# A loop over three batches in all five engines, written out as straight-line code

## What is computed

```python
# layer 0, per batch
x = x + gate_s * (window_attention(modulate(ln(x))) @ w_so + b_so)        # 16 heads of 16, windows of 128, shifted by 64
x = x + gate_c * (topk_cross_attention(modulate(ln(x)), ctx) @ w_co + b_co)  # top 16 of 77 context tokens
x = x + gate_m * (swiglu(modulate(ln(x))) @ w_m2 + b_m2)                  # hidden width 1024
# layer 1, per batch
nx = layer_norm(x); ev = softmax(nx @ keys.T / 16) @ values               # keys, values from the context
h  = concat(nx, ev, cond)
y  = sum_e route[e] * (silu(h @ e_w1[e] + e_b1[e]) @ e_w2[e] + e_b2[e])   # 3 experts, softmax router
y  = y * sigmoid(silu(h @ gate_w1 + gate_b1) @ gate_w2 + gate_b2)
out = x + y @ out_w + out_b
```

## Time and profile before

| what | value |
|---|---|
| median of 3 runs | 1470.52 us (1466.71 to 1470.59) |
| the profiled execution, own time | 1472.61 us |
| its span, first to last instruction | 1470.8 us |
| PE busy | 1419.6 us (97%) |
| DVE, ACT, POOL busy | 69%, 57%, 29% |

### The profile page before, as it was taken

How to read it: one execution, slowest core, us unless ns; L and a number is a source line. 1 busy time by engine, 2 the same in 40 slices (tenths; PEclk the granted TensorE clock), 3 DMA queues, 4 the chain that set the end, 5 groups by cost and what they waited for, 6 DMA issues and landing times.

```text
span 1470.8 us, 33203 instructions
## 1 busy us (share of the span) xinstructions
PE 1419.6 (97%) x9701; PEld 1196.6 (81%) x9701; DVE 1019.0 (69%) x4629; ACT 840.8 (57%) x2554; POOL 427.6 (29%) x613
## 2 busy tenths in 40 slices
PE   6978999999999999999999999999999999999987
PEld 5856888888888788888888788888888888887876
DVE  3384858678695867869596686959587685958532
ACT  3364375756657475665747466574757547574423
POOL 2213232323225232322334232233234313232302
PEclk9878999999999999999999999999999999999989
DMA  7600000010000000010010000000010000000000
GB/s 240 234 30 1 1 1 25 1 34 9 19 30 7 12 2 25 2 33 2 12 45 2 17 2 16 11 14 21 9 47 2 15 2 8 2 2 8 1 8 8
DMA packets 27368, 35.26 MB, mean 24 GB/s; under 512 B 3324, under 2 KB 22448, under 8 KB 26929
## 3 DMA queue, kind: packets, MB, share of 16 engines
q1 hardware_dynamic: 27185, 33.07, 7.2%
HBM read 28.83 MB, written 4.22 MB: 22 GB/s over the span
## 4 chain that ended last, share of the span: by engine, by line
PE 81%; DVE 12%; issue 4%; ACT 2%; DVEq 0%; SPq 0%; DMA 0%; POOL 0%; ACTq 0%; POOLq 0%
PE bank L932 14%; PE bank L956 12%; PE bank L887 11%; PE bank L939 7%; PE bank L760 6%; PE bank L819 5%; PE bank L896 4%; PE bank L807 4%; PE bank L871 3%; DVE knocked L2125 3%; PE bank L746 3%; PE bank L799 2%; PE bank L717 2%; DVE M L2113 2%; PE bank L731 1%
## 5 line engine op out<-in xcount | busy, mean ns | idle before, releaser
L887 PE MATMUL bank<-hB,Wm 128*128 128x256 f32 x1024 | 243.8, 384 | 4.4 <-issue 3.1
L887 PEld LDWEIGHTS bank<-hB,Wm 128*128 128x128 f32 x1024 | 191.2, 191 | 36.5 <-issue 12.4
L932 PE MATMUL bank<-nxT,W1nx 128*128 128x256 f32 x896 | 214.7, 386 | 0.0
L1341 ACT ACTIVATE prob<-bank,rmax 128x128 f32<-128x128 f32 x512 | 180.4, 434 | 30.6 <-DVE rmax L2073 30.6
L1348 ACT ACTIVATE probT<-bank 128x512 f32<-128x512 f32 (+1 forms) x256 | 140.2, 616 | 91.1 <-PE bank L871 77.9
L1684 POOL TENSOR_TENSOR scores<-scores,M 128x308 f32<-128x308 f32 x128 | 94.4, 737 | 331.0 <-DVE knocked L2125 331.0
L932 PEld LDWEIGHTS bank<-nxT,W1nx 128*128 128x128 f32 x896 | 168.2, 193 | 24.0 <-issue 2.8
L956 PE MATMUL bank<-W2p,gT 128*128 128x256 f32 x768 | 184.6, 384 | 2.9 <-DVE acc L2204 1.9
L956 PEld LDWEIGHTS bank<-W2p,gT 128*128 128x128 f32 x768 | 141.9, 191 | 24.1 <-issue 2.8
L1377 ACT ACTIVATE tbs<-bank,b1half 128x256 f32<-128x256 f32 x128 | 60.7, 474 | 148.1 <-PE bank L887 99.3
L1389 ACT ACTIVATE tbs<-bank,betaH 128x256 f32<-128x256 f32 x224 | 95.6, 489 | 82.4 <-PE bank L939 82.4
(11 more groups left out here) (223 smaller groups left out, 2715.7 us busy)
## 6 DMA issues: line engine op xcount, KB each, us to landing
Wm_g<-in_L_xcond_w_m_dram SPq DMA_DIRECT2D x4, 1024.0 KB, 6.0
W1ev<-in_L_xcond_e_w_dram SPq DMA_DIRECT2D x6, 512.0 KB, 7.6
x<-in_x_dram SPq DMA_DIRECT2D x16, 128.0 KB, 2.2
x<-in_x_dram SPq DMA_DIRECT2D x32, 64.0 KB, 2.7
Wm<-in_L_xcond_w_m_dram SPq DMA_DIRECT2D x1, 2048.0 KB, 9.3
out_dram<-acc SPq DMA_DIRECT2D x16, 128.0 KB, 1.7
out_dram<-acc SPq DMA_DIRECT2D x32, 64.0 KB, 2.0
batch_rows<-row_store SPq DMA_DIRECT2D x4, 384.0 KB, 4.1
```

Of the source, the lines that this page charges most:

```text
L887: m = pe.matmul(bank_of(name)[:, half * UT:(half + 1) * UT], Wm1[:, k, c:c + P], hB[:, k, :], start=(k == 0), stop=(k == CB - 1))
L932: pe.matmul(bank_of(name)[:, n * UT:(n + 1) * UT], W1nx[:, k, c0 + n * P:c0 + (n + 1) * P], nxT[:, k, :], start=(n == 0 and k == 0), stop= ...
L1341: m = act.activation(prob[:, s, i, :], psum[s][:, i * P:(i + 1) * P], ACT.Exp, bias=rmax[:, t, s * HPS + i:s * HPS + i + 1], accum_out=rsu ...
```

## The change

The hardware loop becomes a Python loop in all five engines. The body is then emitted three times, q (or b) is 0, 1 and 2, and every wait value, DMA offset and batch index in it is a constant. Nothing else differs: the order of the work, the tiles, the semaphores, the prologue and the passes behind the loop are the same.

```diff
@@ SyncE
-            with sp.Fori(0, NB - 1) as b:
+            for b in range(NB - 1):
                 for r in range(1, UNITS + 1):
                     both(b * UNITS + r, r % UNITS, b)
                     load_x(b * UNITS + r + UNITS - 1, r - 1)
@@ TensorE
-            with pe.Fori(0, NB - 1) as q:
+            for q in range(NB - 1):
                 for r in range(1, UNITS + 1):
                     both(q * UNITS + r, r % UNITS, q + r // 3)
@@ ScalarE
-            with act.Fori(0, NB - 1) as q:
+            for q in range(NB - 1):
@@ GpSimd
-            with pool.Fori(0, NB - 1) as q:
+            for q in range(NB - 1):
@@ VectorE
-            with dve.Fori(0, NB - 1) as q:
+            for q in range(NB - 1):
```

## The result

The changed kernel takes 1466.32 us in the median of 20 runs (1460.61 to 1469.31), the kernel before 1471.07 us in 20 runs (1466.71 to 1475.45). The ratio is 0.9965, 95% interval 0.9955 to 0.9975: faster by 5.1 us, 3.7 to 6.6 us (the two medians are 4.75 us apart). I had forecast 1462.6 us, 7.9 us less. The direction was right and the time lies in the range, but about a third of the gain is missing.

The account below looks back on a forecast made before the run. PE, busy 97% of the span, was taken to bound the kernel. Returns of 3.46 us plus constants of 4.4 us gave 7.9 us off the 1470.52 us median: 1462.6 us, range 1458.0 to 1467.5 us.

Parts of the forecast that it names:

- What bounds it: Whole span: PE is busy 97% of it and carries 81% of the chain, so only waits of PE count.
- Part 1: PE before L887, at the loop's two returns: 1.71 and 1.75 us of issue wait go away, 3.46 us.
- Part 2: All loop passes: constant wait values end small delays, chiefly on DVE before its pick L2132; 4.4 us over three iterations.
- 0.15 us of r = 1: Loop passes with r = 1: what constants gain per pass beyond the return, 0.15 us in each of 3 passes.
- r = 2: Loop passes with r = 2, no return among them: constants gain 0.38 us each, 82.10 to 81.72 us.
- r = 3: Loop passes with r = 3, no twin behind the loop: gain bounded by nothing and 0.93 us, taken as 0.5 us.
- r = 0: Loop passes with r = 0, no twin behind the loop: gain bounded by nothing and 0.54 us, taken as 0.45 us.
- Rival A: Only returns pay; fewer DMA loads explain the faster r = 2 pass behind the loop: 1467.1 us, 12% chance.
- What is added: Body written three times: no added work or wait, and no more code fetched, since the loop is fetched anew each iteration.
- Rival B: Straight-line code starves PE at block borders, 1.73 us per missed fetch: 1567 us if all 60 stall, 3% chance.
- The sum: Whole kernel: returns 3.46 us plus constants 4.4 us, a gain of 7.9 us, to 1462.6 us.
- Rival C: Last pass: granted clock drops while PE idles, some 2.4 us lost in one place; changes the number only, no chance given.

Follow-up runs that it names:

- e1: Kernel before with only TensorE's loop written out, the other four engines keeping theirs: ratio 0.9974 to before, 925.96 us from first to twelfth L1420.
- e2: Kernel before with only VectorE's loop written out: ratio 0.9997 to before, 927.52 us from first to twelfth L1420.
- near loop: Changed kernel plus a four-iteration loop of one semaphore increment on TensorE at both former return places: r = 1 passes take 90.49 and 89.99 us.
- e7: The changed kernel run once more, unchanged: ratio 0.9967 to the kernel before, 923.77 us from first to twelfth L1420.

## Why the prediction was right, and where it was short

- **What bounds it**: right. PE's busy time fills the passes after the change as before.
- **Part 1, the returns, 3.46 us**: right. e1 shows them gone, e2 shows them staying (1.61 and 1.50 us idle), and the near loop shows that it is not the branch as such. The size was of one execution: the idle time at a return is 1.10 to 1.66 us over ten. That the other engines' returns are hidden holds: ScalarE's is 2.06 us and costs nothing.
- **Part 2, the constants, 4.4 us**: the mechanism is right in the main, the pace of VectorE before the pick, shown by e2. I had put all of it on VectorE; e1 shows that about 0.1 us a pass is TensorE's own wait values. This is also the 0.15 us of r = 1, for with VectorE's loop kept that pass is at 89.65 us already. r = 2 was put at 0.38 us and gave 0.41, 0.51 and 0.40. r = 3, at 0.5, gave 0.53, 0.28 and 0.53. r = 0, at 0.45, gave 0.72, 0.41 and 0.32. The 11 passes after the first were to give 7.8 us and gave 6.7. Rival A is refuted by the r = 2 passes of the changed kernel: with the loads beside them they take 81.59 to 81.71 us.
- **What is added: no work and no wait**: this is the step that failed. Straight-line code on VectorE has stalls of its own, and in the r = 1 passes one came at a place where PE waits for what hangs on it: 90.51 and 90.01 us instead of 89.69, 0.82 + 0.32 = 1.1 us. That is the whole miss in these 11 passes; r = 2, 3 and 0 together came out 0.1 us better than forecast. In the first pass two more cost 0.6 us where I counted 0.15 us of gain. Rival B had a stall of straight-line code, but on the wrong engine. I priced it by TensorE's return and dismissed it by TensorE's busy time; the stalls are on VectorE, at 0.2 to 0.5 us, one of them stretched to 0.82 us by GpSimd's longer L1678 behind it.
- **Outside the span**: counted as unchanged, it took 0.7 us.
- **The first pass**, from its first L887 to L1420, was 89.94 us before and 90.52 us after, and pairs at like clock give the same 0.5 to 0.6 us of loss. (It is 88.88 us in e7, the changed kernel at a granted clock of 1.00 from 128 us on, so single profiles compare only at like clock.)
- **The sum**: 6.7 us in the 11 passes, less 0.6 us in the first and 0.7 us outside, is 5.4 us, in the interval of 3.7 to 6.6 us around the measured 5.1. The last 0.3 us is below what these runs can settle: the first L1420 alone scatters from 221.7 to 227.7 us over the 14 profiles.
- **Rival C, the clock**: it goes with the time of single executions, as said, but I looked for it in the last pass. The larger part of the scatter is there by the first L2100, in three groups of start times for three values of the granted clock in the first 59 us. Holding it up from 70 us on gained nothing, at the price of added matmuls on the chain.

## What to carry to other kernels

Where a kernel has a loop and also runs the same body behind it, the trace holds the experiment already: compare the passes, and split the difference at the return by the timeline of the engine that bounds. Then write out only the engines whose returns or wait values are on the path; here TensorE and VectorE gave all of it. Straight-line code is not free either: look for small gaps on the engines that issue many short instructions, without a releaser or behind the engine's own result, and count the instructions between them. Here they stood at multiples of 128 from each other, so a shift only chooses which instructions they fall on.

## What was not expected of the hardware

- A loop's return, 2366 matmuls back, cost TensorE 1.71 and 1.75 us, and left it idle for 1.10 to 1.66 us over ten returns in five profiles; ScalarE's left it idle for 2.06 and 2.12 us in e1. Three returns to the instruction before left no gap on TensorE.
- A register-computed wait value delays VectorE's next short instruction by 0.08 us at one place, and e2 without them has r = 2 passes shorter by 0.4 to 0.5 us.
- VectorE's straight-line code has gaps of 0.15 to 0.5 us, all at instructions whose number is 63 more than a multiple of 128. They fall on other work when 50 or 100 instructions are put in front, at the same total.
- GpSimd's L1678 takes 1.01 to 1.07 us in the eight cases in which it starts while VectorE runs L2149, and 0.71 or 0.72 us in the other 769.
- TensorE held at full clock from 100 to 128 us (1.00 instead of 0.68) by added matmuls made the kernel no faster (1.0003); the added matmuls themselves were on the chain.
- The granted clock of the first 59 us (0.86, 0.88 or 0.94) sorts the 14 profiles by when VectorE's first L2100 starts: 64.8 to 65.9, 62.3 to 63.1 and 59.3 to 59.7 us.
